# The mixer of a decoder kernel: a sibling's order of steps at the start of its loop and around the row statistics

## What is computed

```python
x = x + _L0_attn_ref(_layernorm(x), ...)          # the mixer: the part that is changed
x = x + _L0_xattn_ref(_layernorm(x), ctx, mask)
x = x + _L0_ffn_ref(_layernorm(x), ...)           # top-k routed FFN
x = x + _L1_attn_ref(_layernorm(x), ...)
x = x + _L1_xattn_ref(_layernorm(x), ctx)         # fp8-like quantisation
x = x + _L1_ffn_ref(_layernorm(x), ...)           # ternary weights

def mamba3_forward(u, ...):
    proj = layer_norm(u) @ in_proj_w.T             # z, x, B, C, dt
    B, C = rms_norm(B), rms_norm(C)
    dA = softplus(dt + dt_bias) * -exp(A_log)
    y = ssd_chunked(x, dA, B, C) + x * D           # decay matrix exp(segsum(dA)), running state
    return u + (y * silu(z)) @ out_proj_w.T
```

## Time and profile before

| | us |
|---|---|
| median of three timed runs | 1146.19 |
| lowest and highest of them | 1145.49, 1148.26 |
| the profiled execution | 1143.97 |
| its span in the trace | 1142.1 |
| mixer | from 0 to about 500 |
| mean granted TensorE clock | 0.971 |

### The profile page before, as it was taken

The page is one execution under the profiler, slowest core; times in us unless marked ns, Lnnn a source line. Parts: engine busy times, 40 slices in busy tenths (PEclk is TensorE's granted clock), DMA queues, the critical chain, the costliest instruction groups (busy, mean ns, idle before and its releaser), DMA issues.

```text
span 1142.1 us, 14677 instructions
## 1 busy us (share of the span) xinstructions
PE 1039.7 (91%) x4830; PEld 744.6 (65%) x4830; DVE 829.9 (73%) x1583; ACT 633.8 (55%) x1233; POOL 468.7 (41%) x727
## 2 busy tenths in 40 slices
PE   5779999999999999869998959997889999999896
PEld 4667887888778888645455548775656566666442
DVE  5676776777767767724866748858887988979873
ACT  4634444444444443225564447474468989898773
POOL 5344323432343233223786512305554554735420
PEclk9899999999999999989999979999999999999898
DMA  8200000000000000134110006430001111111123
GB/s 298 92 1 1 1 1 1 1 1 1 1 1 1 1 1 1 38 140 189 77 38 1 1 28 249 141 118 1 1 6 22 32 36 43 38 41 40 32 62 79
DMA packets 48427, 52.91 MB, mean 46 GB/s; under 512 B 34529, under 2 KB 35553, under 8 KB 46049
## 3 DMA queue, kind: packets, MB, share of 16 engines
q1 hardware_dynamic: 48352, 51.99, 14.3%
HBM read 39.92 MB, written 4.19 MB: 39 GB/s over the span
## 4 chain that ended last, share of the span: by engine, by line
PE 56%; DVE 17%; POOL 11%; issue 8%; ACT 7%; DMA 1%; POOLq 0%; DVEq 0%; ACTq 0%
PE bank L405 44%; PE bank L490 3%; PE bank L413 3%; DVE cum_h L904 2%; PE bank L481 1%; POOL wq L2245 1%; POOL wq L2249 1%; PE bank L471 1%; DVE prod L1348 1%; DVE half_lo L1238 1%; POOL wq L2255 1%; POOL wq L2238 1%; PE bank L501 1%; DVE a_st L822 1%; DVE y L940 1%
## 5 line engine op out<-in xcount | busy, mean ns | idle before, releaser
L405 PE MATMUL bank<-win_hi,a_uT_hi 128*128 128x512 f32 (+1 forms) x320 | 130.2, 407 | 7.3 <-DVE win_lo L855 4.0
L405 PE MATMUL bank<-win_lo,a_uT_hi 128*128 128x512 f32 (+1 forms) x320 | 122.4, 382 | 0.0
L405 PE MATMUL bank<-win_hi,a_uT_lo 128*128 128x512 f32 (+1 forms) x320 | 122.0, 381 | 0.0
L1589 ACT ACTIVATE ex<-bank 128x48 f32<-128x48 f32 x16 | 3.3, 209 | 150.8 <-PE bank L449 150.8
L2131 POOL TENSOR_TENSOR y<-y,off 128x512 f32<-128x512 f32 x24 | 37.8, 1573 | 114.1 <-DVE off L925 114.1
L405 PEld LDWEIGHTS bank<-win_hi,a_uT_hi 128*128 128x128 f32 x320 | 62.6, 196 | 22.1 <-issue 6.4
L405 PEld LDWEIGHTS bank<-win_lo,a_uT_hi 128*128 128x128 f32 x320 | 62.6, 196 | 13.5 <-issue 2.9
L405 PEld LDWEIGHTS bank<-win_hi,a_uT_lo 128*128 128x128 f32 x320 | 62.1, 194 | 11.9
L405 PE MATMUL bank<-wq,eT 128*128 128x512 f32 x128 | 62.9, 637 | 6.6 <-ACT eT L1883 6.5
L490 PEld LDWEIGHTS bank<-xs,wgt 128*128 128x128 f32 x512 | 61.1, 192 | 6.9 <-issue 5.7
L405 PE MATMUL bank<-f,fqT_next 128*128 128x512 fp8e4 (+1 forms) x312 | 64.0, 362 | 1.5 <-DMA fqT_next<-fq 1.5
(11 more groups left out here) (335 smaller groups left out, 3047.2 us busy)
## 6 DMA issues: line engine op xcount, KB each, us to landing
wchunk<-w_in SPq DMA_DIRECT2D x32, 256.0 KB, 4.9
stage<-f_in SPq DMA_DIRECT2D x4, 1408.0 KB, 6.0
x<-x_in SPq DMA_DIRECT2D x16, 256.0 KB, 6.2
land<-win_in SPq DMA_DIRECT2D x4, 1024.0 KB, 8.7
wq<-ctxT_in SPq DMA_DIRECT2D x4, 1024.0 KB, 8.4
ctx<-ctx_in SPq DMA_DIRECT2D x4, 1024.0 KB, 5.9
out<-x SPq DMA_DIRECT2D x16, 256.0 KB, 2.0
first_stage<-f_in SPq DMA_DIRECT2D x2, 1408.0 KB, 14.9
```

What stands on the lines that cost most here:

```text
L405: made = e.matmul(bank, a, b, start=start and n == 0, stop=stop and n == len(pairs) - 1)
```

## The change

On TensorE, `running(0)` stands ahead of `project(0, 4)`. On ScalarE, `high_cum(0)` and `shape_cum(0)` stand ahead of the first and the second `tanh_z` of tile 0. On VectorE, `low_cum(0)` stands ahead of `gate_z(0, 0)` and the four `spread_cum(0, q)` ahead of the loop, while `gate_z(0, 1)` goes into round 1, to where these spreads were; and `a_stats` of the groups 2, 3 and 4, in rounds 1, 5 and 9, moves from the end of the round to ahead of `gate_z(i, 1)`. On GpSimd, in round 1, `skip_y(0)` follows `decay_logs(1)` instead of standing ahead of it. No instruction is added or removed.

```diff
@@ tensor_program
             turn_un(1)
+            running(0)
             project(0, 4)
-            running(0)
@@ vector_program
+            low_cum(0)
             gate_z(0, 0)
-            gate_z(0, 1)
-            low_cum(0)
+            for q in range(NG):
+                spread_cum(0, q)
             for i in range(1, NT + 2):
...
                 if i == 1:
-                    for q in range(NG):
-                        spread_cum(0, q)
+                    gate_z(0, 1)
...
                 if old:
                     low_yT(k, 1)
+                if i + 3 < NT and (i + 3) % TPB == 0:
+                    a_stats((i + 3) // TPB + 1)
                 if new:
                     gate_z(i, 1)
...
                     spread_cum(i, 3)
-                if i + 3 < NT and (i + 3) % TPB == 0:
-                    a_stats((i + 3) // TPB + 1)
                 if old:
                     add_mixed(k)
@@ scalar_program
             scale_x(0)
+            high_cum(0)
             tanh_z(0, 0)
+            shape_cum(0)
             tanh_z(0, 1)
             scale_x(1)
-            high_cum(0)
-            shape_cum(0)
@@ gpsimd_program
-                if mix:
+                if mix and i > 1:
                     skip_y(m)
                 if new:
                     decay_logs(i)
+                if i == 1:
+                    skip_y(m)
```

## The result

The changed kernel took 1137.51 us (median of four runs, 1136.95 to 1139.02) against 1145.84 us for the kernel before, measured beside it: ratio 0.9929, 95% interval 0.9906 to 0.9952. Over all of them the changed kernel's 16 runs have a median of 1138.7, and the 62 runs of before made beside these and the experiments one of 1145.6: 6.9 us faster. The 8.3 us between the first two medians are thus more than the kernel keeps.

What follows compares the result with a forecast made beforehand. TensorE, busy for 91% of the span, was taken to bound the kernel except at a few waits, with round 1 set by the other engines; 5.67 + 1.20 + 1.20 = 8.07 off 1146.19 gave 1138.1 us, range 1135.5 to 1142.5.

Steps and rivals of the forecast that it cites:

- round 1 hangs on the chain over the other engines: Round 1: a chain crossing ScalarE, GpSimd and VectorE, not TensorE, sets when round 2 begins.
- Part 1: Start of the mixer: tile 0's sums, shaping and spreads earlier; exp_sums(0) near 38.95, chain gains 1.15 us, not 2.23.
- Part 2: Round 1, GpSimd: skip_y(0) behind decay_logs(1) closes 3.16 us before running(1); y_product(0, 1) ends 4.4 us earlier.
- Part 3 and the unknown price: VectorE, rounds 1, 5, 9: a_stats fills idle time; slowing of bn_stats beside weigh_xs nothing or 1.69 us, taken as nothing.
- `turn_un(3)` 5.67 us earlier: End of round 1: add_state(0) at 67.26 instead of 72.93, turn_un(3) behind it 5.67 us earlier.
- Rounds 5 and 9: 1.20 each: VectorE's end of these rounds comes 1.35 earlier; TensorE had waited 1.20, so each gains 1.20 us.
- rival 2: A new wait, port sharing or low clock around turn_un(3), keeps part of the gain; 4.5 to 6.5 us gained; chance 0.20.
- What is won is not given back to a transfer: Mixer: loads of this phase landed by 36 us, later ones follow the mixer's progress; no gain lost to them.
- The median lies 2.2 above the profiled execution: Whole kernel: timed median 2.2 us above the profiled execution, carried over, giving 1146.19 us as the start.
- 1 falls: TensorE's closed waits count in full: 9.84 us gained, giving 1136.3; chance 0.10.
- 3 falls: Nothing measurable: something later sets the pace, rounds 5 and 9 are bound by TensorE; 0 to 3 us gained; chance 0.12.
- 4 did not come near: Slower: TensorE stays at 1.2 GHz after idling before turn_un(3), deciding from 18 us on; 30 us gives 1152.3; chance 0.03.

Runs made afterwards that it cites:

- Part 1 alone: Kernel before with only running(0), the shaping and spreading of tile 0 and gate_z(0, 1) in their new places; 1143.32 us, ratio 0.9983.
- first profile: Profiled execution from the changed kernel's first measurement, all moves in; that measurement's median was 1137.51 us, ratio 0.9929.
- second and third: Profiles of the changed kernel measured again twice without any edit; 1139.74 us, ratio 0.9954, and 1138.5 us, ratio 0.9935.
- part 2 alone: Kernel before with only skip_y(0) moved behind decay_logs(1) on GpSimd in round 1; 1142.94 us, ratio 0.9979.
- part 3 alone: Kernel before with only a_stats moved ahead of gate_z(i, 1) in rounds 1, 5 and 9; 1142.04 us, ratio 0.9970.

## Why the prediction was right, and where it was off

- *TensorE's few waits are what can be won; round 1 hangs on the chain over the other engines.* Right. Part 1 alone closed a wait of 2.23 us and gained 1.21.
- *Part 1: 1.15.* It was 1.2 to 1.4. The reason was half right: `exp_sums(0)` came at 37.97, a microsecond sooner than worked out, mostly because the low clock on `project(0, 4)` ended sooner (its 512-column matmuls took 4.33 us together, where before they took 5.01); ScalarE then waited 0.59 for `normal(2)`, behind the spreads. So VectorE's spreads, not the sums, set the front now, and the 0.61 before `turn_un(2)` is the same wait on TensorE. I had seen neither.
- *Part 2: `y_product(0, 1)` ends near 58.3, `weigh_xs(0)` at 58.4.* Measured were 57.95 and 58.12. `running(1)` came at 53.14, without a wait.
- *Part 3 and the unknown price.* `a_stats` worked out to start at 57.67 and began at 57.41; `gate_z(1, 1)` worked out for 60.47, measured 60.33; `add_state(0)` 67.26 and 67.09. The price that no row had shown, `bn_stats` beside `weigh_xs`, is zero for both of them, the bound that I had taken.
- *`turn_un(3)` 5.67 us earlier.* Measured 5.68, of which 0.11 was an earlier start of everything.
- *Rounds 5 and 9: 1.20 each.* 28.37 became 27.02, 1.35 each. The 0.15 over is in how the wait was counted. Before, `turn_un(7)` started 1.68 behind the `decay` matmul ahead of it (187.60 to 189.28), of which the profile calls 1.20 idle; now it starts 0.33 behind it (183.34 to 183.67), before that matmul's recorded end (0.49 long). A wait that closes gives back this overlap too.
- *The term that was mis-sized is the clock, which the forecast put at nothing.* In the first profile it cost 1.38 behind `turn_un(3)`, which was rival 2's mechanism at its price of about 1.5, only that the 0.82 of wait before `turn_un(4)`, which was to hide most of it, was used up as well; in the second and third it cost 1.8 and 1.0 ahead of `turn_un(3)` (71.19 and 70.40, less 69.11 and less the 0.25 and 0.30 us by which these executions began later), in a place that I had not named. At `turn_un(15)` the first profile is 417.18 - 410.21 = 6.97 ahead, where the terms had 8.07. With all measurements together 6.9 us were gained, between the forecast (7 to 9) and rival 2 (4.5 to 6.5): the order of steps gives what the forecast said, and the low clock, at one place or another, takes one to nearly two us of it.
- *What is won is not given back to a transfer.* No load shows as a releaser in this stretch. But the spans of the two profiles differ by 4.9, not 6.97. Of the missing 2.1 us, 0.8 went in the last rounds of the mixer, behind `turn_un(15)`: `add_mixed` of a late tile, in the kernel before and then in the changed one, lies 6.18 us apart.

```profile
491.39 0.69 DVE L983 SCALAR_TENSOR_TENSOR x<-bank,x 128x512 f32<-128x512 f32 x1 [2.92 <-PE bank L405]
```
```profile
485.21 0.69 DVE L983 SCALAR_TENSOR_TENSOR x<-bank,x 128x512 f32<-128x512 f32 x1 [2.91 <-PE bank L405]
```

The clock was 0.57 from 476 to 480 us in the one and 0.53 from 468 to 475, a longer stretch, in the other. The remaining 1.3 went in stages that the change does not touch. Stretches of low clock lie at different places there, such as this one of the changed kernel, where the kernel before had 1.00:

```profile
808.00:813.00 5.00, 4.53 (x13) 3.60 (x14) 3.00 (x5) 0.24 (x1) 0.00 (x0) 0.66 0.00 0
```

I did not fill the waits there, so that such stretches make up the difference is argued, not shown.
- *The median lies 2.2 above the profiled execution.* That step has no basis: the profile of before was one of its quicker executions. In the changed kernel's first measurement the profiled execution, at 1139.02, was the slowest of four. That 1138.1 was predicted and 1138.7 measured over all runs is in part luck: the start was 0.6 too high (1146.19 for 1145.6) and the gain 1.2 too large (8.07 for 6.9), and the two pull against each other.
- *Rivals.* 1 falls (part 1 alone, and 6.13 us of waiting in part 2 alone). 3 falls with rounds 5 and 9, and with 6.9 us gained. 4 did not come near: it needed 18 us of low clock, and the longest low stretch in the three profiles of the changed kernel, up to `turn_un(15)`, was about 7 us; in the second profile it lengthened TensorE's work in round 1 by 2.8 (from the second half of `y_product(0, 0)` to `y_product(0, 1)` 9.79 instead of 6.96).

## What to carry over

Before moving a step, follow the chain over all engines to the next point where everything meets, here `normal(3)`, and count only what arrives there; a closed wait on the busiest engine does not say what is won (2.23 closed, 1.2 won). Look also at which steps the move brings side by side on VectorE and GpSimd: more than half of part 2's gain was two operations that no longer collided. And take more than one profile before trusting a microsecond: where TensorE waits, its clock may fall, at another place in each execution. Matmuls that nobody needs, put into such waits, took 2.6 us off the kernel before.

## What the runs showed of the hardware

- TensorE's low clock comes around its waits, but not reproducibly. Past 40 us, three profiles of one kernel had it at 70 to 76 us behind 4.35 us of waiting; at 49 to 56 and 63 to 70, around waits of 1.63 and 2.22; and at 50 to 55 and 71 to 75, behind waits of 1.63 and 3.31. With the larger waits of the start filled, 20 to 106 us ran at 1.00. The Trainium skill (TensorE: Matmul & The Clock Gate, "HAM oscillation") has a kernel that waits between blocks of work run each block from the low level up again; here equal waits had a low stretch in some cases and in others none: 3.16 us before `running(1)` in part 3 alone (0.51) but not in the kernel before (1.00), 1.63 inside `y_product(0, 0)` in two of the three profiles.
- Four `bn_stats` took 2.47 us alone and 2.47 us with a GpSimd multiply of 1.90 us beside them for 1.76. A VectorE multiply with two SBUF inputs beside the same step went from 1.28 to 2.99 for two, and the split of `wout` from 2.28 to 2.96.
